# One expert's surplus rows in a mixture-of-experts kernel: a 32-row tile in plain fp32 and four column groups, computed before the expert's weights are split

## What is computed

```
probs = softmax(x @ gate_w.T); w, idx = top_k(probs, 2); w = w / sum(w)
combine = zeros(T, 8).at[token, idx].add(w)
for e in range(8):
    g, u = split(x @ gate_up[e].T)                        # 256 -> 2 x 1024
    out += combine[:, e] * ((silu(g) * u) @ down[e].T)    # 1024 -> 256
x = x + tanh(g_ffn) * out
```

## Time and profile before

| | us |
|---|---|
| device time, median of 3 executions | 581.39 |
| lowest and highest | 581.28, 582.18 |
| span of the profiled execution (first to last instruction) | 580.4 |
| TensorE busy in it | 555.3 |
| VectorE, ScalarE, GpSimd busy | 396.9, 320.6, 277.2 |

### The profile page before, as it was taken

The page is one execution under the profiler, slowest core; times in us unless marked ns, Lnnn a source line. Parts: engine busy times, 40 slices in busy tenths (PEclk is TensorE's granted clock), DMA queues, the critical chain, the costliest instruction groups (busy, mean ns, idle before and its releaser), DMA issues.

```text
span 580.4 us, 13544 instructions
## 1 busy us (share of the span) xinstructions
PE 555.3 (96%) x5542; PEld 479.8 (83%) x5542; DVE 396.9 (68%) x759; ACT 320.6 (55%) x632; POOL 277.2 (48%) x237
## 2 busy tenths in 40 slices
PE   8999999999989999999999999998999999989994
PEld 7776767777757788988988898877999999979993
DVE  7887568678778576767567755766576767746752
ACT  3554554564574667566555656556266656626631
POOL 3567647757730165567756546722104224421423
PEclk9999999999999999999999999999999999999998
DMA  7910840000000000000000000037365566716111
GB/s 257 361 45 2 323 190 3 2 2 2 2 2 1 2 1 2 10 17 8 19 9 25 9 18 17 9 125 328 80 253 177 171 193 245 263 27 238 28 25 21
DMA packets 24090, 50.92 MB, mean 88 GB/s; under 512 B 7072, under 2 KB 17104, under 8 KB 20688
## 3 DMA queue, kind: packets, MB, share of 16 engines
q1 hardware_dynamic: 18560, 45.20, 21.5%
q0 software_dynamic: 4224, 3.70, 3.6%
q10 hardware_dynamic: 1232, 1.01, 0.6%
HBM read 37.89 MB, written 13.31 MB: 88 GB/s over the span
## 4 chain that ended last, share of the span: by engine, by line
PE 72%; POOL 13%; DVE 7%; issue 3%; ACT 2%; DMA 2%; POOLq 0%; DVEq 0%; ACTq 0%
PE ps L59 15%; PE ps L60 14%; PE ps L61 14%; POOL sr L1866 6%; PE ps L751 4%; PE ps L769 4%; PE ps L739 4%; POOL P L1928 3%; PE ps L608 3%; DVE KN L1141 3%; PE ps L626 3%; PE ps L642 2%; PE ps L587 2%; POOL xs L1938 1%; PE ps L545 1%
## 5 line engine op out<-in xcount | busy, mean ns | idle before, releaser
L1928 POOL TENSOR_SCALAR P<-P,rinv 112x487 f32<-112x487 f32 x56 | 88.6, 1597 | 45.8 <-DVE rinv L1184 44.9
L425 POOL DMA_INDIRECT out<-WS,rows_i x16 | 28.7, 1791 | 90.4 <-ACT WS L1769 86.8
L59 PE MATMUL ps<-XGf,WH 128*128 128x256 f32 x252 | 71.3, 283 | 0.0
L60 PE MATMUL ps<-XGf,WH 128*128 128x256 f32 x252 | 71.3, 283 | 0.0
L61 PE MATMUL ps<-XGf,WL 128*128 128x256 f32 x252 | 71.3, 283 | 0.0
L1866 POOL TENSOR_TENSOR sr<-sv,mhalf 125x32 f32<-125x32 f32 x13 | 70.7, 5436 | 1.1
L1141 DVE TENSOR_REDUCE KN<-ps 112x4 f32<-112x1500 f32 x32 | 55.0, 1719 | 19.0 <-PE ps L608 18.8
L1501 DVE TENSOR_TENSOR WL<-WR,WH 128x1024 fp32r<-128x1024 f32 x48 | 57.1, 1218 | 14.2 <-ACT WH L1823 10.0
L1685 ACT ACTIVATE P<-ps,nm 112x487 f32<-112x487 f32 x64 | 42.0, 664 | 25.4 <-DVE nm L1176 25.4
L1622 ACT ACTIVATE P<-ps 125x1344 f32<-125x1344 f32 x32 | 41.4, 1293 | 21.4 <-PE ps L626 20.9
L1823 ACT ACTIVATE WH<-WR 128x1024 fp32r<-128x1024 f32 x48 | 48.7, 1049 | 0.1
(11 more groups left out here) (282 smaller groups left out, 1537.9 us busy)
## 6 DMA issues: line engine op xcount, KB each, us to landing
WR<-in_gupT SPq DMA_DIRECT2D x16, 1024.0 KB, 7.4
WR<-in_dwnT SPq DMA_DIRECT2D x8, 1024.0 KB, 10.2
xs<-ZT SPq DMA_DIRECT2D x14, 516.0 KB, 6.1
CT<-in_ctxT SPq DMA_DIRECT2D x1, 2250.0 KB, 10.0
P<-xs SPq DMA_DIRECT2D x7, 256.0 KB, 10.8
P<-xs SPq DMA_DIRECT2D x9, 128.0 KB, 2.3
Wk<-in_L_xattn_Wk SPq DMA_DIRECT2D x2, 512.0 KB, 11.2
Wv<-in_L_xattn_Wv SPq DMA_DIRECT2D x2, 512.0 KB, 11.1
```

Of the source, the lines that this page charges most:

```text
L59: e.matmul(out, ah, bh, start=start, stop=False)
L60: e.matmul(out, ah, bl, start=False, stop=False)
L425: return e.indirect_dma_start(result, rows, src, None, bounds_check=NT - 1, oob_is_err=False, compute_op=ALU.add)
L1928: e.tensor_scalar(P[:, k, 0:487], P[:, k, 0:487], rinv[:, k:k + 1], None, ALU.mult).then_inc(s("psc"), 1)
```

## The change

The surplus rows of an expert are cut into a tile of 32 rows (256 to 287), computed by a new function; rows from 288 on go the old general way (`far`, tiles of 128 rows, now five instead of four for each expert). The core of the diff:

```
+SMALL = 32
+FAR_FROM = 2 * 128 + SMALL
...
-    put("ahead", 0)
+    put("ahead", 1)
...
+    def past_inline(x, then):
+        put("over", x)
+        put("oversent", x)
+        if then < NE:
+            put("ahead", then)
...
             if pdc == 3:
-                put("rows", p)
-                if p == NE - 1:
-                    put("oversent", p)
+                if p == 0:
+                    put("rows", 0)
                 put("sent", p)
-                put("over", p)
-                if p < NE - 1:
-                    put("oversent", p)
-                if p + 1 < NE:
-                    put("ahead", p + 1)
+                if p == 0:
+                    past_inline(0, 2)
...
+        if i < len(units) and dc == 1 and x + 1 < NE:
+            put("rows", x + 1)
+            past_inline(x + 1, x + 2 if x else 0)
...
+        def tensor_small(e, w, x):
+            weights = [WR[x % 3]] if x else [f_(WH[0]), f_(WL[0])]
+            groups = [slice(SMALL * g, SMALL * g + SMALL) for g in range(4)]
+            banks = small_banks(x)
...
+            for k in range(2):
+                t = e.transpose(banks[1][:, k * SMALL:(k + 1) * SMALL], XG[0:SMALL, 4, k * 128:(k + 1) * 128],
+                                ident[0:SMALL, 0:SMALL])
...
+            w.wait_ge(act, 4 * n + 1)
+            for part in range(2):
+                for k, W, g in itertools.product(range(2), weights, range(4)):
+                    o = k * 2048 + part * 1024 + g * 256
+                    t = e.matmul(banks[part][groups[g], :], XS_[:, k, :], W[:, o:o + 256],
+                                 start=(k == 0 and W is weights[0]), stop=(k == 1 and W is weights[-1]),
+                                 tile_position=(0, SMALL * g))
+                t.then_inc(pe, 1)
+            w.wait_ge(dve, 2 * n + 1)
+            for c in range(2):
+                t = e.transpose(banks[0][:, c * 128:(c + 1) * 128], H_[:, c * 128:(c + 1) * 128], ident[:, :])
...
+            w.wait_ge(act, 4 * n + 3)
+            for c, W, g in itertools.product(range(2), weights, range(4)):
+                o = 4096 + (2 * g + c) * 256
+                t = e.matmul(banks[1][groups[g], :], HS_[:, c, groups[g]], W[:, o:o + 256],
...
+            w.wait_ge(dve, 2 * n + 2)
...
+            e.matmul(ps[0:SMALL, 6, 0:256], fold[:, :], YP_, start=True, stop=True).then_inc(pe, 1)
...
         def split_low(e, w, x, c):
+            if x:
+                w.wait_ge(s("over_pe"), 6 * moe.n("over", x))
...
+        def scalar_small(e, w, x):
...
+            e.activation(XS_, banks[1][:, 0:2 * SMALL].rearrange("p (k n) -> p k n", k=2), ACT.Copy).then_inc(act, 1)
...
+            e.activation(G_, banks[0], ACT.Silu).then_inc(act, 1)
...
+            e.activation(HS_, banks[0].rearrange("p (c n) -> p c n", c=2), ACT.Copy).then_inc(act, 1)
...
+            if n:
+                w.wait_ge(s("tile_y"), 16 * n)
...
+            e.activation(YSo[0:SMALL, :], ps[0:SMALL, 6, 0:256], ACT.Copy, scale=EX[0:SMALL, x, 2, 0:1]).then_inc(act, 1)
...
+            x = before("sent", *entry) - 1
             if x >= 0:
                 for t_ in range(2):
                     w.wait_ge(s(f"y{2 * (x % 2) + t_}"), 16 * (x // 2 + 1))
-                w.wait_ge(s("tile_y"), 16 * (x + 1))
+            if before("oversent", *entry):
+                w.wait_ge(s("tile_y"), 16 * before("oversent", *entry))
```

More of the change, by code:

```diff
@@ L25 @@
 ROW = D + 2
+SMALL = 32
+FAR_FROM = 2 * 128 + SMALL
+FAR_TILES = [(FAR_FROM + 128 * k, min(128, NT - FAR_FROM - 128 * k)) for k in range(-(-(NT - FAR_FROM) // 128))]
+NFAR = len(FAR_TILES)
 class Order:
@@ L434, in build @@
         YSo = PTf[:, 3072:3328]
+        fold = sb("fold", [128, SMALL])
+        XS_ = XTf[:, 0:2 * SMALL].rearrange("p (k n) -> p k n", k=2)
+        HS_ = XTf[:, 64:320].rearrange("p (c n) -> p c n", c=2)
+        H_, YP_, G_ = (HS[:, 256 * k:256 * k + 256] for k in range(3))
         YS = cols(2048, 4, 256)
@@ L908, in tensor_experts @@
                             if t_ == 1:
-                                w.wait_ge(s("tile_act"), 6 * x)
+                                w.wait_ge(s("over_act"), 4 * before("over", stage, *i))
                         for c2 in range(2):
@@ L945, in counts, with load_counts @@
             return [count_of(e, w, x) for x in range(NE + 1)]
+        def load_counts(e, w, count, x, dc):
+            if (x, dc) == (0, 2):
+                count[0] = count_of(e, w, 0)
+            if dc == 0 and x + 1 < NE:
+                count[x + 1] = count_of(e, w, x + 1)
         def count_of(e, w, x):
@@ L949, in count_of, with nth, before, next_pair @@
             return e.value_load(cnt[0:1, x:x + 1], min_val=0, max_val=NT)
+        def nth(stage, x):
+            return moe.n(stage, x) - 1
+        def before(what, *entry):
+            return sum(q[0] == what for q in moe.entries[:moe.entries.index(entry)])
+        def next_pair(x):
+            return max(u for q, u in pair_use.items() if moe.entries.index(q) < moe.entries.index(("over", x))) + 1
+        def small_banks(x):
+            return [ps[:, bk, 0:256] for bk in PAIRS[next_pair(x) % 3]]
         def pairs_out(w, x):
@@ L1968, in pool_experts @@
                     x, = i
[L1969 to L1971 removed]
+                    added(w, stage, x)
+                    w.wait_ge(s("over_act"), 4 * moe.n("over", x))
+                    rows = bass.IndirectOffsetOnAxis(ap=rows_i[0:SMALL, x, 2:3], axis=0)
+                    scatter_add(e, rows, YSo[0:SMALL, :]).then_inc(s("tile_y"), 16)
                     if x == 0:
```

172 lines of the change are left out of this document (95 added, 77 removed).

## The result

The changed kernel takes 575.8 us (median of 4 runs, 575.6 to 575.9) where the kernel before takes 581.7 on the same chip (4 runs, 581.3 to 582.2). The ratio is 0.990, with a 95% interval of 0.9886 to 0.9914: **faster by 1.0%, 5.9 us**. The forecast was 576.3. The profiled execution has a span of 574.1 us where the one before had 580.4.

A forecast was written before the change was run, and what follows sets the result against it. TensorE's gapless instruction stream was taken to bound the expert phase. 581.39 us less 4.9 for the shorter tile (11.64 to 6.7) and 0.2 at the end gave 576.3 us, range 574.9 to 578.3.

The forecast's parts named there:

- What is removed: Expert 4's surplus tile in TensorE's stream: its whole 11.64 us goes, as nothing runs beside it on TensorE.
- Step 1: New tile's start, from the end of down(2, 3): change of shape, transposed rows, ACT's 64-column copy, hand-over; 0.93 us.
- Steps 2 and 6: New tile's gate and up products (32 passes, 8 steps), 2.08 us; its down products (4 steps), 1.16 us.
- Steps 3, 4, 5, 7: New tile's DVE product 0.51, two transposes 0.44, ACT's copy 0.38 + 0.09, DVE's copy of four partial products 0.42 + 0.09.
- Step 8: New tile's end: sum of partial products by fold, with change of shape, 0.64 us; then TensorE is free.
- Sum: New tile's whole length on TensorE: 6.7 us, bounds 6.1 to 8.1, against 11.64; 4.9 us gained.
- What else moves, free: Around the tile: earlier weights and count reads, split_low's wait, fold's reduction; no price, at most 0.4 us for expert 0's count.
- The end: POOL's last scatter can start sooner without the last tile's scatter: 0 to 1.0 us, taken as 0.2 us.
- Rival, the clock falls in the tile: At the new tile, TensorE's clock falls to half rate, losing 1.7 us; 578.0 us, chance 0.16.
- Rival, POOL's chain: Scatters waiting for each other reach TensorE at the tile, costing nothing to 6 us; 579.3 at the middle, chance 0.05.
- Rival, groups in turn at 256 columns: In the new tile's products, column groups don't run together; tile 14.7 us, kernel 584.3 us, chance 0.03.
- Rival, `far`: If expert 4 had over 288 rows, they go through far, with loads and tiles at the end; over 640 us, chance 0.01.

The follow-up runs named there:

- e1: Changed kernel with the new tile never entered (branches ask for more than 288 rows), all else kept; 567.68 us.
- e2: Kernel before with the old tile never entered (branches ask for more than 288 rows); 568.86 us.
- e4: Changed kernel with expert 7's surplus scatter put back in POOL's order ahead of expert 7's two scatters; 574.41 us.
- e9: Changed kernel with the small tile on split weights behind its own expert's last down product, and POOL's old wait rule; 578.66 us.
- e7: Changed kernel with the small tile put back behind its own expert's last down product, on split weights, POOL's changed waits kept; 582.34 us.
- e6: Changed kernel with all products of the new tile in column group 0, issued group by group, output overwritten; 584.27 us.
- e5: Changed kernel itself, unaltered, measured again beside others on one chip; 576.05 us, ratio to before 0.9908.

## Why the prediction was right, step by step

The forecast of 576.3 us was met with 575.8, and its reason, the tile's length on TensorE one for one, is shown by e1 and e2. The gain that it forecast was 5.1 us; the traces show 5.3 and the medians 5.9, so the mechanism accounts for all but the half microsecond that stays open.

- **What is removed.** 11.64 us by the earlier trace rows, 11.66 by e2. Right.
- **Step 1**, 0.93: measured 477.67 - 476.84 = 0.83. The step counted the change of shape twice. ACT's copy starts 0.37 us behind the start of its scaling in both kernels, and the scaling starts 0.32 us behind the last matmul of `down`. So the copy comes 0.69 us behind that matmul before (512.64 to 513.33) and now (476.72 to 477.41). The 0.09 us only moved the first transpose closer to it, 0.48 us instead of 0.57.
- **Steps 2 and 6**, 2.08 and 1.16: measured 1.93 and 1.07. The mis-sized terms: a step takes 0.216 us, not 0.23, and the first pass of a piece costs 0.02 more, not 0.09. The 0.09 was the longest pass of L817, a full-width form; I took it over to the narrow form, which has its own rows in L642 (284 against 259 ns, 0.025). That was the row to use.
- **Steps 3, 4, 5, 7**, 0.51, 0.44, 0.47, 0.51: measured 0.55, 0.44, 0.47, 0.55. The copy and the product of 256 columns are the old tile's; DVE starts 0.07 to 0.08 us behind TensorE's last pass where I had 0.045.
- **Step 8**, 0.64: measured 0.55, but the first matmul of the next unit is then followed 0.10 us late, which my sum did not have. The two cancel.
- **Sum** 6.7 (6.74 unrounded): measured 6.39 up to the next unit, 6.5 with what follows. Gain 5.2, not 4.9. Within my bounds of 6.1 to 8.1, of which the lower one comes to 6.2 when its own terms are added up. The changes of shape are five and not six, three of them at waits; the sum has the other two, as it should.
- **What else moves, free**: right; the middles of e1 and e2 agree to 0.03 us. That includes the reads, `split_low`'s wait and the counts of experts 1 to 7. For expert 0's count, which I had bounded at 0.4 us, and for the reduction of `fold` no price shows, but the starts scatter by as much.
- **The end**, 0.2: POOL starts 0.15 us sooner behind the block, in all nine profiles with the changed kernel's waits and its order or e4's. The number is right, the reason only in part. Had the delay counted from the block in the kernel before, nothing would have been gained. In the three profiles where the last surplus scatter stands just ahead of the blocks, POOL starts 1.14 us (before), 1.14 us (e2) and 1.15 us (e9) behind the end of that scatter. In the changed kernel it starts 0.88 us behind the end of DVE's scaling (565.14 to 566.02); before, that distance was 1.03. So before, POOL's own way set the start, and now the block does. In e9 the surplus scatter takes 1.49 us and not 1.74, and POOL starts 1.28 us behind DVE's start: there a shorter scatter in the old order gives as much as the new order does.
- **Rival, the clock falls in the tile**: it stayed at 1.00 with the array at work for 4.39 of 6.39 us. It falls in the routing stretch in some executions of both kernels and not in others, and at the end.
- **Rival, POOL's chain**: half of it came. POOL's scatters of expert 2's surplus, of expert 1's blocks, of expert 3's surplus and of expert 2's blocks, and ACT's last copy of the tile (changed kernel):

```profile
458.61 1.80 POOL L437 DMA_INDIRECT out<-P,rows_i  x1 [1.74 <-issue]
466.63 1.56 POOL L437 DMA_INDIRECT out<-WS,rows_i  x1 [6.21 <-DMA out<-P,rows_i]
...
473.90 1.35 POOL L437 DMA_INDIRECT out<-P,rows_i  x1 [2.88 <-DMA out<-WS,rows_i]
478.12 1.55 POOL L437 DMA_INDIRECT out<-WS,rows_i  x1 [2.88 <-ACT WS L1852]
...
483.34 0.47 ACT L1897 ACTIVATE P<-ps,EX 32x256 f32<-32x256 f32 x1 [2.33 <-PE ps L1101]
```

  Expert 1's blocks started at 466.63, some 6 us later than their place, behind a surplus scatter that took 7.2 us from issue to landing (6.21 behind the end of its instruction). That is my threshold of some 7 us. But I had given all tiles' scatters one length, and expert 3's landed 2.4 us behind its issue, so the chain had caught up before the tile: expert 2's blocks, at 478.12, waited for ACT alone, and ACT's last copy for TensorE. TensorE never waited. e7 shows the same mechanism at the end of the kernel, where nothing is left to absorb it: 2.7 us. I had looked for it only at the tile.
- **Rival, groups in turn at 256 columns**: no; e6 shows what it would have cost, 7.6 us, where I had 14.7 - 6.7 = 8.0. The page TensorE: Matmul & The Clock Gate of the Trainium skill, Measured speedup vs the span model, has 2.38 times for three column groups (M=32, N=512), 0.79 of the ideal. The trace doesn't agree for four groups at 256 columns: 7.09 / 1.93 = 3.7 times with the last pass in both (0.92 of the ideal), and all four without it. So my sum was right to go by L642.
- **Rival, `far`**: 29 matmuls and transposes at 477 us, no `far`.

## What to carry to other kernels

Where one engine's stream has no gaps, a block's price is its start-to-start length in that stream, and it can be costed from rows of the same shapes to a few per cent; take even a small term (here the first pass's extra) from the row of the same form. When a block must wait on other engines, lay its pieces between independent products: here it gave back 1.9 of 2.0 idle microseconds, and sixteen further skipped branches cost less than 0.1 us together. Rules for which transfers may be in flight together are sized for an order; after moving a piece, look at the kernel's end, where no slack is left.

## What the runs showed of the hardware that I had not expected

- The order of the products over the column groups hardly matters (0.13 us over the tile): four passes of one group in a row let the next group's start almost as if they had been interleaved.
- Four column groups of 32 in plain fp32 at 256 columns have a concurrency of 4.0: 0.216 us for a pass alone and 0.216 us for four together.
- A piece of 32-column tiles in the stream costs more than its passes: 0.09 us where it begins (476.72 to 476.93, where 0.12 is regular), some 0.10 where it ends (482.68 to 483.23 holds two passes, 0.45), and 0.10 us more behind the first matmul after it (483.23 to 483.45). Most of this last 0.10 isn't the narrow tile's: behind the four full-width transposes of `xin` in the kernel before it is 0.09 (498.29 to 498.50).

```profile
497.94 0.60 PE L872 MATMUL ps<-ident,P 128*128 128x128 f32 x4
498.29 0.36 PE L59 MATMUL ps<-WH,HTf 128*128 128x256 f32 x1
498.50 0.28 PE L60 MATMUL ps<-WL,HTf 128*128 128x256 f32 x1
```

- The middle of the kernel repeats to 0.03 us across chips. The medians of the kernel before differ by up to 2.5 us between chips, 579.5 to 581.9. It was profiled on one of them only, but in e4 on the chip with the 579.5 the changed kernel's middle is the same 146.90, and the start is 1.6 us sooner than in e5.
